# First cross-attention's norm taken per group inside the self-attention loop, weight splits between its gelus, transposes stored by pairs

## The reference, cut to what matters

```
h  = layernorm(x + attn(...))               # self-attention block
x  = x + h_block + gelu(h @ W1 + b1) @ W2   # last step of the block, per group of 4 sequences
z  = layernorm(x)                           # the norm that the change moves
q  = z @ Wq * DH**-0.5                      # 16 heads of 64
k, v = ctx @ Wk, ctx @ Wv                   # 361 rows per sequence
x  = x + softmax(q k^T) v @ Wo + bo
```

## Time and profile before

| | us |
|---|---|
| median of 3 runs | 1484.53 |
| profiled execution, whole | 1487.75 |
| its span | 1486.0 |
| TensorE matmul busy | 1283.6 (86%) |
| VectorE busy | 1038.8 (70%) |
| ScalarE busy | 739.6 (50%) |
| GpSimd busy | 252.7 (17%) |

### The profile page before, as it was taken

One profiled execution on the slowest core, in us unless ns is written; L12 is line 12 of the kernel. 1 busy time (PEld: TensorE's weight loads), 2 busy tenths in 40 slices (PEclk: granted clock), 3 DMA queues, 4 the chain that ended last, 5 costly groups with the idle time before them and its releaser, 6 DMA issues.

```text
span 1486.0 us, 27736 instructions
## 1 busy us (share of the span) xinstructions
PE 1283.6 (86%) x9826; PEld 1092.9 (74%) x9826; DVE 1038.8 (70%) x2584; ACT 739.6 (50%) x1807; POOL 252.7 (17%) x312
## 2 busy tenths in 40 slices
PE   4889799896899999999999999999879978969319
PEld 4879788785778777877778787777667756759308
DVE  5865466643667776777777677777579976885974
ACT  4442423334565555555555555565446643426463
POOL 3335262524000000000000000000044422000100
PEclk9899899997899999999999999999789988989759
DMA  9000101030100000000000000000020011300001
GB/s 279 30 22 1 43 1 43 1 121 24 44 11 11 6 7 11 10 11 10 11 10 0 11 10 11 10 0 2 1 57 2 2 66 56 98 14 1 0 0 45
DMA packets 34547, 40.66 MB, mean 27 GB/s; under 512 B 4889, under 2 KB 29066, under 8 KB 34442
## 3 DMA queue, kind: packets, MB, share of 16 engines
q1 hardware_dynamic: 33614, 39.24, 8.7%
q10 hardware_dynamic: 828, 0.14, 0.1%
HBM read 35.36 MB, written 4.01 MB: 26 GB/s over the span
## 4 chain that ended last, share of the span: by engine, by line
PE 49%; DVE 18%; issue 6%; ACT 5%; DVEq 0%; POOL 0%; ACTq 0%; POOLq 0%
PE bank L745 8%; PE bank L746 7%; PE bank L747 7%; PE bank L952 4%; PE bank L936 4%; PE bank L944 3%; PE bank L912 2%; ACT prob L1576 2%; DVE amax L2359 2%; DVE nmx L2176 2%; PE bank L1168 1%; PE bank L1186 1%; DVE kTl L2072 1%; PE bank L973 1%; DVE prob L2193 1%
## 5 line engine op out<-in xcount | busy, mean ns | idle before, releaser
L1576 ACT ACTIVATE prob<-bank,nmx 100x361 f32<-100x361 f32 x256 | 142.7, 560 | 163.4 <-DVE nmx L2176 159.9
L2176 DVE TENSOR_REDUCE nmx<-bank 100x1 f32<-100x361 f32 x256 | 124.3, 527 | 22.3 <-PE bank L936 15.3
L671 POOL TENSOR_TENSOR frstd<-fmoments,eps 100x1 f32<-100x1 f32 x32 | 6.2, 194 | 672.1 <-DVE fmoments L2119 672.0
L745 PE MATMUL bank<-cxTh,wxkh 128*128 128x362 f32 x256 | 99.7, 390 | 2.7 <-DVE kTl L2072 2.7
L952 PEld LDWEIGHTS bank<-pT,vv 128*64 128x64 f32 (+1 forms) x1536 | 71.2, 139 | 38.3 <-issue 28.9
L952 PE MATMUL bank<-pT,vv 128*64 128x100 f32 (+1 forms) x1536 | 96.6, 261 | 2.4 <-DVE oTl L2071 2.4
L2193 DVE TENSOR_SCALAR prob<-prob,rsum 100x361 f32<-100x361 f32 x256 | 92.9, 405 | 4.5
L2071 DVE TENSOR_TENSOR oTl<-bank,oTh 128x100 fp32r<-128x100 f32 x128 | 32.9, 257 | 86.7 <-ACT oTh L1562 69.6
L745 PE MATMUL bank<-wxvh,cxTh 128*128 128x512 f32 (+1 forms) x192 | 84.5, 440 | 8.6 <-DVE vv L2100 8.6
L944 PE MATMUL bank<-ident,prob 100*128 100x100 f32 (+1 forms) x768 | 90.2, 253 | 1.6 <-DVE prob L2193 1.6
L944 PEld LDWEIGHTS bank<-ident,prob 100*128 100x128 f32 (+1 forms) x768 | 85.1, 152 | 7.0 <-DVE prob L2193 2.6
(11 more groups left out here) (388 smaller groups left out, 3796.4 us busy)
## 6 DMA issues: line engine op xcount, KB each, us to landing
cx<-in_ctx_dram SPq DMA_DIRECT2D x32, 128.0 KB, 2.1
xc<-in_ctx_dram SPq DMA_DIRECT2D x32, 128.0 KB
parked_weights<-parking SPq DMA_DIRECT2D x9, 256.0 KB, 5.6
mask_i<-in_mask_BxS_ik_dram SPq DMA_DIRECT2D x16, 141.0 KB
w<-in_L_attn_W_dram SPq DMA_DIRECT2D x2, 1024.0 KB, 13.6
cx<-in_ctx_dram SPq DMA_DIRECT2D x16, 105.0 KB, 2.0
xc<-in_ctx_dram SPq DMA_DIRECT2D x16, 105.0 KB
x<-in_x_dram SPq DMA_DIRECT2D x4, 400.0 KB
```

Source lines behind the costliest of these rows:

```text
L745: pe.matmul(o, wh, mh, start=start, stop=False)
L1576: nc.scalar.activation(prob[:, h % 4, :], bank[S_BANKS[e]][0:T, 0:S], ACT.Exp, bias=nmx[:, h:h + 1], accum_out=psum_[:, h:h + 1]).then_inc ...
L2176: nc.vector.tensor_reduce(nmx[:, h:h + 1], bank[S_BANKS[e]][0:T, 0:S], AX_X, ALU.max, negate=True).then_inc(xa_max, 1)
```

## The change

- `zT` becomes [128, 8, 2, 200]: for each pair of sequences the two channel tiles stand side by side. All readers and writers follow. `moments`, `std` and `rstd` become tensors of their own; `kTl` and `vv` move ahead of `wxkh` with 176 columns between.
- VectorE takes the new `rows_stats(g - 1)` right behind `sums_added(g - 1)` in groups 1 to 3, ScalarE the square root (`rows_deviation`) just ahead of its other one. The statistics of group 3 come in the prologue after the first key, their root from GpSimd (add and power).
- In group 3's hidden loop: TensorE transposes the first context into banks 0 and 1 after step 1, and groups 0 and 1 of the normalised rows after steps 3 and 5. ScalarE makes the context's high part, the three weights' high parts (steps 2 to 4), the scaling (step 5) and the copies to `zT` between its gelus. VectorE normalises groups 0 and 1 into `u0` and makes the low parts. GpSimd makes `wxol` right behind its last split, without waiting for `l0_x`.
- Groups 2 and 3 are normalised, transposed and copied in the prologue, by way of `prob` and `pT`.
- SyncE issues the first context ahead of the last weights and the second behind the first's transposes; the other loads still wait for `l0_x`.

```diff
-        zT = sb("zT", [P, KD, B * T])
+        zT = sb("zT", [P, B // 2, KD, 2 * T])
@@ SyncE
             sp.wait_ge(l0_proj, 4 * STEPS)
+            load_ctx(0)
             for name, dst in (("L0_xattn_Wk", wxk), ("L0_xattn_Wv", wxv)):
...
-            sp.wait_ge(l0_x, NG)
-            load_ctx(0)
             sp.wait_ge(xa_ct, KD)
             load_ctx(1)
+            sp.wait_ge(l0_x, NG)
             sp.dma_start(mirror[:], a["mirror"]).then_inc(relb_in, 16)
@@ GpSimd
-            pool.wait_ge(l0_x, NG)
...
+            pool.wait_ge(xa_wh, 3)
+            nc.gpsimd.tensor_tensor(wxol[:], wxo[:], wxoh[:].bitcast(F32), ALU.subtract).then_inc(xa_bv, 1)
+            pool.wait_ge(l0_x, NG)
             bv = vec[:, COL["L0_xattn_bv"]:COL["L0_xattn_bv"] + KC].unsqueeze(2).broadcast_to([P, KC, T])
             nc.gpsimd.tensor_copy(oTh[:], bv).then_inc(xa_bv, 1)
-            pool.wait_ge(xa_bv, 1)
+            pool.wait_ge(xa_bv, 2)
             nc.gpsimd.tensor_tensor(oTl[:], bv, oTh[:].bitcast(F32), ALU.subtract).then_inc(xa_bv, 1)
-            pool.wait_ge(xa_wh, 3)
-            nc.gpsimd.tensor_tensor(wxol[:], wxo[:], wxoh[:].bitcast(F32), ALU.subtract).then_inc(xa_bv, 1)
+            pool.wait_ge(var_ready, TURN[1])
+            nc.gpsimd.tensor_tensor(rstd_all[:, last_rows], moments_all[:, last_rows, 1], ..., ALU.add)
+            nc.gpsimd.tensor_tensor(rstd_all[:, last_rows], rstd_all[:, last_rows], ..., ALU.pow).then_inc(std_ready, 1)
@@ TensorE, hidden loop
                     if c > 1:
                         hidden_summed(first + c - 2)
+                    if not follows and c == 1:
+                        context(0, 0, bank[0])
+                        context(0, 1, bank[1])
+                    if not follows and c in (3, 5):
+                        pe.wait_ge(ln_z, (c - 1) // 2)
+                        if c == 5:
+                            pe.wait_ge(ln_done, KD)
+                        transposes(u0, 2, ln_t)
...
-            pe.wait_ge(l0_x, NG)
-            all_transposes(1)
@@ TensorE, prologue
             pe.wait_ge(xa_bv, 3)
-            context(0, 0, bank[W_BANK])
-            context(0, 1, bank[T_BANKS[0]])
+            pe.wait_ge(l0_x, NG)
             output_product(bank[V_BANK])
             pe.wait_ge(xa_wl, 2)
             pe.wait_ge(xa_cl, KD)
+            pe.wait_ge(ln_done, 2 * KD)
...
+                if c == 4:
+                    pe.wait_ge(xa_cl, 2 * KD)
+                    group_transposes(2, prob, (W_BANK, T_BANKS[0]))
...
+                if c == 7:
+                    pe.wait_ge(ln_done, 3 * KD)
+                    group_transposes(3, pT, (W_BANK, T_BANKS[0]))
+            pe.wait_ge(ln_done, 4 * KD)
@@ ScalarE
+                if g:
+                    rows_deviation(4 + 2 * g, g - 1)
+                deviation(turn_of_hidden(g))
...
+                    if not follows and c == 1:
+                        context_high(0, 0, 0, bank[0])
+                        context_high(0, 1, 0, bank[1])
+                    if not follows and c in (2, 3, 4, 5):
+                        act.wait_ge(wx_in, 64)
+                        if c == 2:
+                            nc.scalar.copy(wxkh[:], wxk[:]).then_inc(xa_wh, 1)
+                        if c == 3:
+                            nc.scalar.copy(wxvh[:], wxv[:]).then_inc(xa_wh, 1)
+                        if c == 4:
+                            nc.scalar.copy(wxoh[:], wxo[:]).then_inc(xa_wh, 1)
+                        if c == 5:
+                            nc.scalar.mul(wxq[:], wxq[:], DH ** -0.5).then_inc(xa_wq, 1)
+                    if not follows and c in (4, 6):
+                        for k in range(KD):
+                            act.wait_ge(ln_t, KD * (c - 4) // 2 + k + 1)
+                            rows_out((c - 4) // 2, k, 2 + k)
...
+                if c in (5, 7):
+                    g = 2 if c == 5 else 3
+                    for k, o in enumerate((W_BANK, T_BANKS[0])):
+                        act.wait_ge(ln_t, KD * g + k + 1)
+                        rows_out(g, k, o)
@@ VectorE
+            def rows_stats(g):
+                dve.wait_ge(l0_x, g + 1)
+                nc.vector.memset(pause[:, 2:3], 0.0)
+                for b in range(G * g, G * g + G):
+                    ins = nc.vector.bn_stats(stats_all[:, b, :], x[:, b, :])
+                link(ins)
+                nc.vector.memset(pause[:, 3:4], 0.0)
+                for b in range(G * g, G * g + G):
+                    ins = nc.vector.bn_aggr(moments_all[:, b, :], stats_all[:, b, :])
+                ins.then_inc(var_ready, 1)
...
                     if c == 3 and g:
                         sums_added(g - 1)
+                        rows_stats(g - 1)
...
                 else:
+                    rows_normalised(0, u0[:].rearrange("t b d -> t (b d)"))
+                    for k in range(KD):
+                        context_low(0, k, 0, bank[k])
+                    weights_rest(0, wxkl, wxk, wxkh)
+                    dve.wait_ge(ln_t, KD)
+                    rows_normalised(1, u0[:].rearrange("t b d -> t (b d)"))
+                    weights_rest(1, wxvl, wxv, wxvh)
                     sums_added(g)
-            norm(1, x)
...
+            rows_normalised(2, rows_of(prob))
             for c in range(PAIRS0):
...
+                if c == 0:
+                    rows_stats(NG - 1)
+                if c == 4:
+                    dve.wait_ge(std_ready, TURN[1])
+                    rows_normalised(3, rows_of(pT))
```

More of the change, by code:

```diff
@@ L840, in hidden, with context @@
                 mm.then_inc(l0_w1, 1)
+            def context(b, k, o):
+                pe.wait_ge(cx_in, 16 * NS * b + 16 * NS)
+                for kt, (k0, r) in enumerate(KS):
+                    mm = pe.transpose(o[:, k0:k0 + r], cx[0:r, kt, k * P:(k + 1) * P], ident[0:r, 0:r])
+                mm.then_inc(xa_ct, 1)
             pe.wait_ge(prep_done, 1)
@@ L907, in keys, with queries @@
                 mm.then_inc(xa_k, 1)
[L909 removed]
+            def queries(c, pair_of_rows, o):
                 for k in range(KD):
[L912 removed]
+                    mm = pe.matmul(o[:, 0:2 * T], wxq[:, k, c * P:(c + 1) * P], zT[:, ds(pair_of_rows, 1), k, :].rearrange("d a q -> d (a q)"),
                                    start=(k == 0), stop=(k == KD - 1))
@@ L998, in pe_pair @@
                     at_least(pe, xa_ol, pair - 2)
-                    queries(p, 2 * T * i + 2 * T, bank[O_BANK])
+                    queries(p, i + 1, bank[O_BANK])
                 if not final:
@@ L1056, in values_slot, with group_transposes @@
                 values_in(kt, half, (odd + ahead_by) % 2, bank[V_BANK])
+            def group_transposes(g, src, banks):
+                flat = rows_of(src)
+                pe.wait_ge(ln_z, g + 1)
+                for k in range(KD):
+                    for t in range(G):
+                        mm = pe.transpose(bank[banks[k]][:, t * T:(t + 1) * T], flat[:, t * D + k * P:t * D + (k + 1) * P],
+                                          ident[0:T, 0:T])
+                    mm.then_inc(ln_t, 1)
             pe.wait_ge(wx_in, 64)
@@ L1395, in _, with rows_out @@
             act.wait_ge(memsets, 2)
+            def rows_out(g, k, b):
+                nc.scalar.copy(zT[:, 2 * g:2 * g + 2, k, :], bank[b][:, 0:N].rearrange("d (a q) -> d a q", a=2)).then_inc(ln_done, 1)
             def all_copies(n, turn):
@@ L1400, in all_copies @@
                         act.wait_ge(ln_t, KD * NG * (n - 1) + KD * g + k + 1)
-                        nc.scalar.copy(zT[:, k, N * g:N * (g + 1)], bank[KD * (g % 2) + k][:, 0:N]).then_inc(ln_done, 1)
+                        rows_out(g, k, KD * (g % 2) + k)
             def first_deviations(turn, first, last):
@@ L1981, in sums_added, with rest, context_low, weights_rest @@
                 ins.then_inc(l0_x, 1)
+            def rest(dst, src, high, bias=None):
+                if bias is None:
+                    return nc.vector.tensor_tensor(dst, src, high.bitcast(F32), ALU.subtract)
+                return nc.vector.scalar_tensor_tensor(dst, src, bias, high.bitcast(F32), ALU.add, ALU.subtract)
+            def context_low(b, k, buf, src):
+                dve.wait_ge(xa_ch, KD * b + k + 1)
+                rest(cxTl[:, buf, k, 0:S], src[:, 0:S], cxTh[:, buf, k, 0:S]).then_inc(xa_cl, 1)
+            def weights_rest(n, low, raw, high):
+                dve.wait_ge(xa_wh, n + 1)
+                rest(low[:], raw[:], high[:]).then_inc(xa_wl, 1)
+            def rows_stats(g):
[8 more added lines that the diff above has]
+                ins.then_inc(var_ready, 1)
+            def rows_normalised(g, dst):
+                if g == 0:
+                    dve.wait_ge(l0_t, KD * NG)
+                    link(nc.vector.reciprocal(rstd_all[:, 0:G * NG - G], std_all[:, 0:G * NG - G]))
+                for t in range(G):
+                    b = G * g + t
```

(19 more changed lines are left out.)

85 lines of the change are left out of this document (42 added, 43 removed).

## The result

| | before | after |
|---|---|---|
| median, us | 1483.61 (1480.54 to 1486.04, 4 runs) | 1468.87 (1467.52 to 1470.03, 4 runs) |
| profiled execution, whole | 1487.75 | 1470.03 |
| its span | 1486.0 | 1468.2 |

The ratio is 0.9901 [0.9879, 0.9924], the brackets being its 95% interval: 14.7 us faster by the medians, 17.8 by the spans of the profiled executions.

What follows compares the result with a forecast made beforehand. TensorE is busy almost throughout, so only its idle stretch between the last row sum and first cross-attention key can shrink. Terms 1.7 + 2.4 - 13.35 + 1.85 = -7.4 gave 1477.0 us from the 1484.53 median, range 1471 to 1483.

Steps and rivals of the forecast that it cites:

- Part 1: Statistics per group: hidden in groups 1 and 3, but in group 2 they stall TensorE's next V projection, +1.7 us.
- the shift of `gated`: In group 2, VectorE's `gated` was to move later by the full 1.85 us of the statistics.
- Part 2: Group 3's hidden loop: transposes on full TensorE, copies on ScalarE; last `hidden_summed` starts 2.4 us later (1.5 to 4.7).
- the 0.83 us that the forecast gave as agreeing: Old normalisation after 374.04: VectorE stood still 0.83 us until GpSimd's `wxol` ended, cited for the SBUF blocking rule.
- Part 3: Between last row sum and first key: `output_product` waits for GpSimd, 14.2 us saved, slow clock +0.85, net -13.35 us.
- the 0.65 that I added for taking turns: Before `output_product`: 0.65 us (0 to 1.3) for `rows_normalised(2)` alternating with GpSimd's `oTh` and `oTl`.
- Part 4: Prologue, first batch's keys and queries: added transposes, statistics and copies cost +1.85 us (1.0 to 3.5).
- The 0.7 for the bias addition: In the prologue, `rows_stats(3)` ahead of the bias addition that the first `values_in` waits for costs +0.7 us.
- Part 5: `zT` by pairs: same columns, matmuls and copies, so nothing gained or lost (bounded by -0.5).
- rival C: Pairs' loop: the four-axis `zT` slice costs a register operation per matmul, making the kernel slower, 1496 us; chance 0.08.
- Rival B: Covers better than charged: no group 2 stall, quick clock return, undisturbed GpSimd, cheaper prologue; -12, 1472.5 us; chance 0.23.
- Rival A: Hidden loop: weight rests block GpSimd splits, TensorE idles about 2 us and its clock falls; -3.4, 1481 us; chance 0.22.

Runs made afterwards that it cites:

- a_stats_late: The changed kernel with group 1's statistics taken one step later in group 2; 1467.03 us, ratio 0.9887 to the kernel before.
- s_splits_pad7: The changed kernel with statistics, root, normalisation and 32 transposes back behind the last row sum, weight splits kept in the hidden loop, 14 met waits added; 1473.60 us, ratio 0.9925.
- n_norm_only: The changed kernel with the weights' high parts, scaling and low parts back behind the last row sum; 1474.91 us, ratio 0.994 to the kernel before.
- a_keys_first: The changed kernel with `output_product` moved behind the second key and query of the prologue; 1461.13 us, ratio 0.985 to the kernel before.
- b_pad7: The kernel before with 14 already met waits (7 instructions) ahead of VectorE's loop over pairs; 1477.83 us against 1483.55, ratio 0.9958.
- b_pad64: The kernel before with 128 already met waits (64 instructions), VectorE's loop starting 860 instructions in; 1475.16 us, ratio 0.9942.
- a_pad121: The changed kernel with 121 more do-nothing instructions ahead of VectorE's loop, 924 in all; 1474.54 us, ratio 0.9952 to the kernel before.

## Why the forecast was right in the seam and wrong in the sum

**Part 1, the stall in group 2: right cause, too large.** Forecast 1.7, the trace shows the wait of 0.71 for `kv` at 227.97, and 0.9 over the whole of group 2 (47.6 for 46.7); *a_stats_late* takes it away. The failed step is the shift of `gated` (its `kv` row): from the row sum to it there are 7.86 us in before (219.46 to 227.32) and 8.96 after (218.32 to 227.28), so 1.10 and not 1.85. One operation of the rounding between them (`blk_scale` from `blk_inv`) took 0.91 in before and 0.18 after, which gives the rest back. In before it stood beside a subtraction of GpSimd (221.60 to 222.67), in after the shift had carried it past the same one (220.46 to 221.51), and in *a_stats_late* it takes 0.91 again. VectorE's and GpSimd's timelines of before, then VectorE's of after:

```profile
221.79 0.91 DVE L1970 SCALAR_TENSOR_TENSOR blk_scale<-blk_inv,delta 128x16 f32<-128x16 f32 x1
```

```profile
221.60 1.07 POOL L609 TENSOR_TENSOR ol<-state,oh 128x400 fp32r<-128x400 f32 x1
```

```profile
222.49 0.18 DVE L2031 SCALAR_TENSOR_TENSOR blk_scale<-blk_inv,delta 128x16 f32<-128x16 f32 x1
```

**Part 2, the hidden loop: right.** Forecast +2.4; from the first `hidden` to the last `hidden_summed` it is 18.96 in before and 21.54 after, +2.6. The blocking by ports was as described: it made one operation of a split 1.48 longer and one 2.45, where the forecast had at most the 2.28 of a rest against a slack of 2.2 to 2.4, and TensorE saw 0.32 of it. *s_splits_pad7* shows what it costs where the rests follow each other; that the normalisation between them is what saves the changed kernel was only argued, since the two differ in the row transposes too.

The Trainium skill, "SBUF — State Buffer", section "Who interferes with whom", says that issue order decides who blocks, not the kind of operation. The trace agrees in both directions: a cast of 0.52 took 2.00 behind a rest that had begun, and four normalisations of 1.4 took 4.26 behind `wxol`. One row does not fit as it stands: the subtraction of 354.07 is recorded 0.32 ahead of the rest of 354.39, and it was the one that was held (3.50 for 1.05), while the rest took its 2.28. And the 0.83 us that the forecast gave as agreeing is of a normalisation, which reads one tensor; the case of two tensor inputs shows in the rests above and in `blk_scale`.

**Part 3, the seam: right.** Forecast -13.35, measured -13.9. GpSimd's chain took 7.48 (362.98 to 370.46) for 8.1: the 0.65 that I added for taking turns was wrong in its direction, since VectorE paid for it (2.86 on the four normalisations) and GpSimd hardly did (0.07 on `oTh`). `output_product` took 4.95 at the lower clock, 4.9 by the forecast. *n_norm_only* moves `wxol` back and moves the product by as much. What I did not draw from my own term is that the wait and its slow clock were to be had: *a_keys_first* got 5.9 us from both.

**Part 4, the prologue: right.** Forecast +1.85, measured +1.25 (18.02 to 19.27). The 0.7 for the bias addition did not show; at the end TensorE waits 0.63 for `zT`.

**Part 5, "Nothing": the step that failed.** For the layout itself it holds: *b_pad7* has the old layout and the changed kernel's rounds, which also refutes rival C: the query matmuls of the loop take 333 ns at the median in before and in after (500 to 980). But the forecast put the whole loop at nothing with it, and took the steady loop as a piece that moves unchanged if no instruction in it changes. It lost 1.1 us in each of five jumps back, -5.5 in all, by seven instructions on VectorE ahead of it; seven empty ones alone gave the kernel before 5.7 (*b_pad7*). The trace of before had the sign, five stops of 3.2 with no releaser at the same line; a price could not have been read from it, but a range could (16.1 us in all, of which *b_pad64* got 8.9 back in its rounds).

With the measured terms the sum is 0.9 + 2.6 - 13.9 + 1.25 - 5.5 = -14.65, and the medians differ by 14.7. That they agree so closely is partly luck, since the spans of the two traces differ by 17.8. Two medians bear the split out without a trace: *b_pad7* has the loop alone (-5.7), *a_pad121* the rest alone (-9.0). Without the loop the sum is -9.2, and 1475.4 would have been in the range. So the range was missed by the one cause that stood in none of its cases. Rival B came nearest, with 1472.5 at -12, for the wrong reasons in part: of its covers the prologue and the undisturbed GpSimd were there and half of the stall, the quick return of the clock was not. Rival A did not come, though its mechanism is real.

**Open:** the start of group 3's `hidden` varies between 334.6 and 340.4 in these traces (its first `hTl`), without relation to the edits, for a part by stretches at the lower clock between 100 and 340. Single profiled executions can so differ by 5 us before the change begins. Of the 3 us between -17.8 and -14.7, 1.6 lie ahead of 342 and the rest behind the loop. The way out of the loop (last row sum to sixteenth `fq`) takes 20.1 to 22.9 us in these traces, and why is open too.

## What to carry to other kernels

When a change adds or removes instructions ahead of a hardware loop, look at the idle time of the first instructions behind the jump back (stops by "issue" in the list of waits are a sign, but a shorter stop can stand under another name), and at the instruction queues' packets: a long body may be loaded anew in each round in one place and not in another, and a few empty instructions move it. Between an engine that ends late and the engine that waits for it, look for work of the waiting engine that can go ahead: it saves the wait and keeps the clock up. And where GpSimd stands in the chain, be wary of two long two-input subtractions of VectorE in a row; one kernel here idled TensorE 1.97 us with them.

## What the runs showed of the hardware that I had not expected

- The place of a loop of 291 VectorE instructions in its stream was worth between 83.4 and 86.9 us a round, and up to 25 packets of 8 KB in the whole run.
- A gap of 1.16 us on TensorE left the granted clock at 1.00 (*a_keys_first*, 363 to 372), while one of 4.80 us did not (0.50 over 370 to 375 in the changed kernel). In the first kernel `output_product` took 2.8 us for 4.95. A gap of 1.97 us (*s_splits_pad7*) was followed by the lower level too (0.57 over 353 to 357).
- A bad place is not bad by the same amount: 84.0, 85.1 and 86.9 at remainders of 35, 28 and 60; at 60 VectorE stopped twice behind each jump.
- Seven empty instructions ahead of a loop that was not touched moved the whole kernel by 5.7 us of 1483.6.
